# A graph kernel with three edits: early roots in the opening, late statistics in the node stage, whole rows in the last stage

## The chip, the cores and the metric

The kernel runs on one core of a Trainium2 chip. The metric is the device time of one execution in microseconds; lower is better. The kernel before was timed three times: 1190.2, 1192.75 and 1195.69 us, median 1192.75 us. Nothing in the text below is a time of the changed kernel.

The core has five engines that run programs of their own and meet at semaphores: TensorE (PE), VectorE (DVE), ScalarE (ACT), GpSimd (POOL) and SyncE (SP). SP here only issues transfers; ACT and GpSimd issue some too. All transfers share 16 DMA engines. `then_inc` raises a semaphore when an instruction is done, `wait_ge` holds the engine's program until a semaphore has reached a value.

## What is computed

`x` has 10,000 nodes of 512 columns, and there are 10,000 edges `src`, `dst` with a weight each. Two layers follow one another, each with a residual and a layer norm (`eps` 1e-5, no scale):

```python
# layer 0: graph convolution with self loops
deg = segment_sum(w, dst) + 1;  d = where(deg > 0, rsqrt(deg), 0)
agg[dst] += x[src] * d[src] * w;  z = agg + x * d          # (aggregated before the product with W)
x1 = layernorm(x + relu((z @ W0) * d + b0))
# layer 1: message passing; an edge takes x1[dst], adds into node src
sj, vj = x1[dst, :128] @ Win_s, x1[dst, 128:].reshape(-1, 128, 3) @ Win_v
u = edge_vec / |edge_vec|;  Yv = Y1 * u
filt = (shifted_softplus(edge_attr @ Wf1 + bf1) @ Wf2 + bf2) * w
# messages: scalar and vector parts from sj, vj, Yv and filt, summed over the edges of a node
S = shifted_softplus(segment_sum(m_s) @ W1_s) @ W2_s;  V = segment_sum(m_v) @ W1_v @ W2_v
out = layernorm(x1 + concat(S, V))
```

## The kernel before, in words

Nodes and edges are padded to 10,240, that is 80 tiles of 128 (`T`), 40 pairs (`T2`), 20 groups of four (`T4`). The five engine programs are written by hand, without a planner; the order of the work is the order of the lines in each program and the waits in them. A function `nodes0(s, u)` is one turn `s` of a stage on one engine, and `live(s, k)` marks the part of it that treats tile `s - k`, so a tile passes through an engine's parts in different turns. `skewed` runs the turns: some unrolled ones, then a hardware loop (`Fori`), then the tail. `held` is a wait with a mark, `Stage` counts marks of one tile.

**Opening.** SP loads the indices and weights (L332 to L346) and the first feature tiles (L353). ACT issues 42 transfers of zeros into `sum0` (L509), 512 KB each, and only then copies `W0h` (L513) and takes the roots of the degrees and of |r|^2 (L515, L516). DVE builds one-hot tiles whose products on TensorE are the degrees (L944), then runs a chain of small dependent steps (`link`): the degrees (L733 to L735), scaled weights, and after ACT's roots the reciprocals, one Newton step and `Y` (L746 to L753). Only then `s_dis` is raised. TensorE waits for it ahead of everything in the edge stage.

**Edge stage 0** (20 groups). GpSimd gathers rows of `x` by `src` (L429). TensorE transposes index columns into rows (L968), DVE compares (L774, L779, L787), picks `d[src]` from a lookup (L1023, L765) and makes `coef`; ACT scales the gathered rows into the high part `G_hi` (L559), DVE makes the low part `G_lo` (L799), TensorE sums rows with equal `dst` in a group (L984), ACT copies the sums out (L544), and GpSimd scatters them with add into `sum0` (L449) at indices from L804. The filter network of layer 1 runs beside it (L1019, L995, L538; written to `filt_d` by SP, L357). The first scatter waits for all 42 transfers of zeros, a group's scatters for those of the group before.

**Node stage** (80 tiles, `nodes0` on each engine). SP loads a tile of `sum0` (`sl`, 4 buffers) and of `x` (`xl`, 8 buffers). DVE: `z = x*d + sum` (L829). ACT: high part (L607). GpSimd: low part (L476). TensorE: four transposes of each part by `ident_r` (L1047). ACT: two copies from PSUM (L595, L600). TensorE: twelve matmuls with `W0h`, `W0l` (L1057). DVE: `*d + b0` (L823), ReLU and residual (L832), statistics (L834, L836), all one after the other on one tile. ACT: Ln and Exp of the variance (L590, L598). GpSimd: five one-column steps (L463 to L472). ACT: normalisation in place (L611). SP: two stores, `x1_d` and columns 128 to 511 of `sum1`. The result buffers `res` are four. ACT also issues zeros for the first 128 columns of `sum1`, and four last ones (L616).

**Edge stage 1** is not touched but for the buffers that it shares.

**Last stage** (40 pairs, `nodes1`). SP loads columns 0 to 127 of `sum1` for two tiles into `ssum` (L402), the other columns into `al` (L410), 128 columns of `x1_d` into `xs` (L412). `pair_rows` puts row `p` of tile `2s` and row `p` of tile `2s+1` on partition `p`. ACT and DVE compute the shifted softplus (L668, L678, L686; L900, L908), TensorE transposes and multiplies (L1121, L1128), DVE adds (L916) and takes statistics (L924, L928), ACT normalises (L657), SP stores 512 KB (L406). `al` has 8 buffers, `ssum` and `xs` 4.

## Time and profile before

| | |
|---|---|
| median of 3 runs | 1192.75 us |
| the profiled execution's own time | 1193.07 us |
| its span | 1191.3 us |
| busy: PE, DVE, ACT, POOL | 1000.9, 835.9, 701.7, 660.3 us |
| opening and edge stage 0 | 0 to 354.7 us |
| node stage, and the fill of edge stage 1 | 354.7 to 686.5 us |
| edge stage 1 | 686.5 to 1044.1 us |
| last stage | 1044.1 to 1191.3 us |
| moved by DMA | 289.00 MB, mean 243 GB/s |

The span is what the profiler saw from the first to the last instruction; the execution's own time has 1.8 us around it. A busy share is an average over stages of different kind, so it says little on what a change of one stage is worth: a stage is read by the period with which its instructions repeat, and by what each waits for. A row of the timeline has start, duration, engine, line, operation, and in brackets the idle time in front and what ended it. PE is TensorE's matmuls; PEclk is the granted share of its clock.

### The profile page before, as it was taken

Reading aid. Unit: us, or ns where it says so; the run is one execution under the profiler, and the core shown is the slowest. Engines: PE = TensorE matmul, PEld = TensorE weight load, DVE = VectorE, ACT = ScalarE, POOL = GpSimd, SP = SyncE. Lnnn points to the kernel's source line nnn. Section 1 sums busy time; section 2 is a strip of 40 time slices with the busy share of each in tenths; the row PEclk is TensorE's granted clock in tenths of the full one; section 3 lists DMA queues with packets and bytes.
Section 4 is the critical chain, followed back from the end, with each engine's and each line's share of the span. In section 5 each row is a group of like instructions: output and inputs, shape, how many; then the busy total and the mean of one; then the engine's idle time right before and its main releaser. Section 6 shows DMA issues by size and latency. Waiting matters only on the chain.

```text
span 1191.3 us, 23227 instructions
## 1 busy us (share of the span) xinstructions
PE 1000.9 (84%) x5088; PEld 790.9 (66%) x5088; DVE 835.9 (70%) x2538; ACT 701.7 (59%) x1632; POOL 660.3 (55%) x812
## 2 busy tenths in 40 slices
PE   7479998998838999999999399999999999634442
PEld 7458777776627888888888267777777777433332
DVE  8578876787606777787777366666666666368887
ACT  0068787777725666666666344444444444268887
POOL 3038888888745777777777546656566664400000
PEclk9999988999878999999999789999999999955555
DMA  9949999999986788878887669999999998589998
GB/s 356 418 156 235 245 228 229 247 253 227 220 170 207 265 276 279 277 277 278 278 277 263 235 161 211 194 202 195 205 194 208 195 205 177 69 256 347 351 351 287
DMA packets 175015, 289.00 MB, mean 243 GB/s; under 512 B 18514, under 2 KB 75750, under 8 KB 174966
## 3 DMA queue, kind: packets, MB, share of 16 engines
q1 hardware_dynamic: 120982, 176.23, 44.2%
q0 software_dynamic: 35840, 83.91, 36.7%
q10 hardware_dynamic: 18144, 28.32, 6.3%
q8 instruction: 17, 0.28, 0.1%
q14 instruction: 32, 0.26, 0.1%
HBM read 139.49 MB, written 148.90 MB: 242 GB/s over the span
## 4 chain that ended last, share of the span: by engine, by line
PE 30%; issue 17%; POOL 11%; DMA 5%; DVE 2%; ACT 2%; POOLq 2%; SPq 1%; ACTq 0%; DVEq 0%
PE bank L1084 6%; PE bank L1095 4%; POOL tiny L463 3%; PE bank L1093 3%; POOL tiny L466 3%; PE bank L1105 3%; PE bank L1107 3%; PE bank L1108 3%; DMA node_mem<-sum 3%; PE bank L1077 2%; PE bank L1085 1%; PE bank L1091 1%; PE bank L1057 1%; POOL tiny L470 1%; POOL tiny L468 1%
## 5 line engine op out<-in xcount | busy, mean ns | idle before, releaser
L500 POOL DMA_INDIRECT sum<-R_mem,l_sidx x80 | 128.0, 1600 | 126.1 <-ACT R_mem L625 74.3
L449 POOL DMA_INDIRECT sum<-R_mem,sidx_all x80 | 133.6, 1670 | 53.1 <-issue 29.1
L1057 PE MATMUL bank<-W0h,G_hi 128*128 128x512 f32 x320 | 134.0, 419 | 1.0 <-ACT G_lo L600 0.9
L1057 PE MATMUL bank<-W0l,G_hi 128*128 128x512 f32 x320 | 126.2, 394 | 0.0
L1057 PE MATMUL bank<-W0h,G_lo 128*128 128x512 f32 x320 | 126.2, 394 | 0.0
L611 ACT ACTIVATE node_mem<-node_mem,tiny 128x512 f32<-128x512 f32 x80 | 65.4, 818 | 91.7 <-POOL tiny L472 91.7
L476 POOL TENSOR_TENSOR G_lo<-node_mem,G_hi 128x512 fp32r<-128x512 f32 x80 | 104.4, 1305 | 17.8 <-ACT G_hi L607 17.8
L880 DVE SCALAR_TENSOR_TENSOR edge_mem<-edge_mem,Y,bank 128x128 f32<-128x128 f32 x240 | 72.5, 389 | 57.4 <-ACT edge_mem L639 57.4
L639 ACT COPY edge_mem<-bank 128x256 f32<-128x256 f32 x80 | 29.9, 373 | 134.3 <-PE bank L1095 134.3
L984 PE MATMUL bank<-G_hi,M_mem 128*128 128x512 f32 x200 | 88.5, 442 | 17.8 <-ACT R_mem L544 17.6
L492 POOL DMA_INDIRECT G_mem<-x_d,dst_i x80 | 79.5, 993 | 35.3 <-issue 23.2
L823 DVE SCALAR_TENSOR_TENSOR node_mem<-bank,dis,b_s 128x512 f32<-128x512 f32 x80 | 60.1, 751 | 54.1 <-DMA sum<-node_mem 46.3
L1121 PE MATMUL bank<-ident,node_mem 128*128 128x128 f32 x80 | 27.4, 446 | 83.8 <-DVE node_mem L908 83.8
L829 DVE SCALAR_TENSOR_TENSOR node_mem<-G_mem,dis,node_mem 128x512 f32<-128x512 f32 x80 | 67.0, 839 | 32.1 <-DMA G_mem<-x 32.1
L1084 PE MATMUL bank<-edge_mem,Winv 128*128 128x512 f32 x160 | 82.9, 600 | 0.5 <-DVE edge_mem L871 0.5
L984 PE MATMUL bank<-G_lo,M_mem 128*128 128x512 f32 x200 | 82.8, 414 | 0.0
L995 PE MATMUL bank<-edge_mem,Wf_s 128*128 128x256 f32 x320 | 81.0, 399 | 1.5 <-DVE edge_mem L808 0.8
L1077 PEld LDWEIGHTS bank<-ident,G_mem 128*128 128x128 f32 x240 | 40.1, 195 | 58.6 <-issue 58.6
L1121 PEld LDWEIGHTS bank<-ident,node_mem 128*128 128x128 f32 x80 | 11.6, 204 | 96.0 <-ACT node_mem L664 52.3
L995 PEld LDWEIGHTS bank<-edge_mem,Wf_s 128*128 128x128 f32 x320 | 65.7, 208 | 13.6 <-issue 2.5
L633 ACT COPY edge_mem<-bank 128x512 f32<-128x512 f32 x80 | 46.9, 587 | 42.1 <-PE bank L1079 42.1
L538 ACT ACTIVATE node_mem<-bank,bf_c 128x256 f32<-128x256 f32 x160 | 63.3, 491 | 14.3 <-PE bank L995 14.2
(172 smaller groups left out, 2953.0 us busy)
## 6 DMA issues: line engine op xcount, KB each, us to landing
sum<-zeros ACTq DMA_DIRECT2D x42, 512.0 KB, 13.7
filt_d<-node_mem SPq DMA_DIRECT2D x40, 512.0 KB, 5.1
node_mem<-sum SPq DMA_DIRECT2D x80, 256.0 KB, 2.8
G_mem<-x SPq DMA_DIRECT2D x80, 256.0 KB, 2.8
x_d<-node_mem SPq DMA_DIRECT2D x80, 256.0 KB, 2.1
node_mem<-filt_d SPq DMA_DIRECT2D x80, 256.0 KB, 4.6
sum<-node_mem SPq DMA_DIRECT2D x80, 192.0 KB, 2.3
out<-G_mem SPq DMA_DIRECT2D x20, 512.0 KB, 4.2
```

Of the source, the lines that this page charges most:

```text
L449: pool.indirect_dma_start(sum0, bass.IndirectOffsetOnAxis(ap=sidx[:, t:t + 1], axis=0), R[t % 8][:, :], None, compute_op=ALU.add).then_inc ...
L476: pool.tensor_tensor(z_lo[u][:, :], sl[u], z_hi[u][:, :].bitcast(F32), ALU.subtract).then_inc(n_lo, 1)
L492: pool.indirect_dma_start(G3[t % 8][:, :], None, x1_d, bass.IndirectOffsetOnAxis(ap=dst_i[:, t:t + 1], axis=0)) \
L500: pool.indirect_dma_start(sum1, bass.IndirectOffsetOnAxis(ap=l1_sidx[:, t:t + 1], axis=0), R3[t % 8][:, :], None, compute_op=ALU.add).then ...
L611: act.activation(res[a], res[a], ACT.Identity, bias=tiny[a][:, 6:7], scale=tiny[a][:, 5:6]) \
L829: dve.scalar_tensor_tensor(sl[c], xl[u], dis[:, bass.ds(s, 1)], sl[c], ALU.mult, ALU.add).then_inc(n_z, 1)
L880: st.mark(dve.scalar_tensor_tensor(mo[:, :, i], msg[c][:, 0:P], Y[:, bass.ds(t, 1), i], bank[6][:, i * P:(i + 1) * P], ALU.mult, ALU.add))
L984: ins = pe.matmul(bank[b][:, :], M[c][q][:, j * P:(j + 1) * P], part_[(4 * g + q) % 8][:, :], start=(q == 3 and part_ is G_hi), stop=(q == ...
L995: ins = pe.matmul(bank[6 + r][:, q * 256:(q + 1) * 256], Wf2_s[:, base:base + 255:2], h[c][:, v * 256:(v + 1) * 256], start=True, stop=True)
L1057: ins = pe.matmul(bank[4 + a][:, :], zt[b][:, c * P:(c + 1) * P], w[:, c, :], start=(c == 0 and k == 0), stop=(c == 3 and k == 2))
L1077: pe.transpose(bank[0][:, i * P:(i + 1) * P], gv[:, :, i], ident[:, :])
L1084: pe.matmul(bank[2][:, :], Winv[:, :], rawT[b][:, 0:512], start=True, stop=True)
```

## The change

Three parts, which touch separate stages.

1. Opening and edge stage 0. ACT issues 8 of the 42 transfers of zeros; SP issues the other 34, behind its loads and the first two feature tiles. ACT waits for the degrees only (`s_const` 4) before the first root. DVE takes the scaled weights and `Y` out of the opening and puts them behind the edge loop; the inverse root follows the first group's counts; TensorE waits for `s_dis` only before the first lookup. In group 0 TensorE and ACT do the first two sums ahead of the next transposes, and DVE makes `M` and `G_lo` ahead of the counts. Gathers share a semaphore by four.
2. Node stage. `z` is transposed once, in fp32; the split into high and low part is made after it (ACT `zT_hi`, DVE `zT_lo`), in four buffers each. ReLU goes to ACT, the residual add to GpSimd, and DVE's statistics follow two turns later. The tail of the statistics (Ln, Exp, GpSimd's steps) runs once for two tiles. Eight `res` buffers, eight store semaphores.
3. Last stage. `node_pair` puts rows `2p` and `2p+1` of 256 on partition `p`, so both are 4 KB in one piece; whole rows of `sum1` go into `al`, whose columns 0 to 127 take the place of `ssum`. `al` has 13 buffers, `xs` 8. Padding rows are neither loaded nor stored. All programs of the stage are unrolled, and a store stands ten turns behind its load.

```diff
+def node_pair(dram, s, c0, c1):
+
+    n = min(256, N - s * 256)
+    return dram[s * 256:s * 256 + n, c0:c1].rearrange("(p k) d -> p k d", k=2)
...
-        al = split(views(0, 4, 2 * D, G_mem) + views(0, 4, 2 * D, R_mem))
-
-        ssum, sr, sp, spT, xs = (split([b[:, q * 2 * C:(q + 1) * 2 * C] for b in node_mem]) for q in range(5))
+        NA = 13
+        al = split(views(0, 4, 2 * D, G_mem) + views(0, 4, 2 * D, R_mem) + views(0, 5, 2 * D))
+
+        sr, sp, spT = (split([b[:, q * 2 * C:(q + 1) * 2 * C] for b in node_mem]) for q in (1, 2, 3))
+        xs = split([b[:, q * 2 * C:(q + 1) * 2 * C] for q in (0, 4) for b in node_mem])
...
+            for s in range(2):
+                sp_.dma_start(fT[s][:, :], rbf[:, s * Q:(s + 1) * Q]).then_inc(w_fT[s], 16)
+            sp_.wait_ge(s_zero, 1)
+            for j in range(NZ, 42):
+                sp_.dma_start(zero_rows(j), zeros[:, :]).then_inc(s_zero0, 16)
...
-                if live(s, 8):
-                    t = s - 8
+                if live(s, 12):
+                    t, a = s - 12, (u - 12) % 8
                     held(sp_, n_x1, t + 1)
...
+            for s in range(T2 + 10):
+                if s < T2:
+                    if s >= NA:
+                        sp_.wait_ge(g_st[(s - NA) % 8], 16 * ((s - NA) // 8 + 1))
+                    if s >= 8:
+                        sp_.wait_ge(g_res, K_RES4 * (s - 8) + 1)
+                    sp_.dma_start(pairs_in(al[s % NA], s), node_pair(sum1, s, 0, D)).then_inc(g_al[s % 8], 16)
+                    sp_.dma_start(pairs_in(xs[s % 8], s), node_pair(x1_d, s, 0, C)).then_inc(g_xs[s % 8], 16)
+                if s >= 10:
+                    t = s - 10
+                    sp_.wait_ge(g_y, 2 * (t + 1))
+                    sp_.dma_start(node_pair(out, t, 0, D), pairs_in(al[t % NA], t)).then_inc(g_st[t % 8], 16)
...
+                if live(s, 7) and u % 2 == 0:
+
+                    t, a = s - 8, u // 2
+                    g = t // 2 if isinstance(t, int) else (t - u) // 2 + a
+                    w, mean, var = tiny[a], mv[a][:, :, 0], mv[a][:, :, 1]
+                    st = Stage(n_rstd, g, K_ROOT)
+                    held(pool, n_mv, t + 2)
+                    st.mark(pool.tensor_scalar(w[:, 0, :], var, EPS, None, ALU.add))
+                    st.mark(pool.tensor_scalar(w[:, 7, :], mean, -1.0, None, ALU.mult))
+                    held(pool, n_rs, 2 * (g + 1))
+                    st.mark(pool.tensor_tensor(w[:, 3, :], w[:, 2, :], w[:, 2, :], ALU.mult))
+                    st.settle(pool)
+                    st.mark(pool.tensor_tensor(w[:, 4, :], w[:, 3, :], w[:, 0, :], ALU.mult))
                     held(pool, n_rstd, st.reached())
-                    held(pool, n_rs, 2 * (t + 1))
-                    st.mark(pool.tensor_scalar(w[:, 3:4], w[:, 2:3], w[:, 2:3], w[:, 0:1], ALU.mult, ALU.mult))
-                    held(pool, n_rstd, st.reached())
-                    st.mark(pool.tensor_scalar(w[:, 4:5], w[:, 3:4], -0.5, 1.5, ALU.mult, ALU.add))
+                    st.mark(pool.tensor_scalar(w[:, 3, :], w[:, 4, :], -0.5, 1.5, ALU.mult, ALU.add))
                     st.settle(pool)
-                    st.mark(pool.tensor_tensor(w[:, 5:6], w[:, 4:5], w[:, 2:3], ALU.mult))
-                    held(pool, n_rstd, st.reached())
-                    st.mark(pool.tensor_scalar(w[:, 6:7], mean, w[:, 5:6], -1.0, ALU.mult, ALU.mult))
-                if live(s, 0):
-                    pool.wait_ge(n_hi, s + 1)
-                    wait(pool, n_tr, s - 3)
-                    pool.tensor_tensor(z_lo[u][:, :], sl[u], z_hi[u][:, :].bitcast(F32), ALU.subtract).then_inc(n_lo, 1)
-
-            skewed(pool, nodes0, 6, 8)
-
-
-            for u in range(4):
-                held(pool, n_st[u], 32 * (T // 4))
+                    st.mark(pool.tensor_tensor(w[:, 5, :], w[:, 3, :], w[:, 2, :], ALU.mult))
+                    st.settle(pool)
+                    st.mark(pool.tensor_tensor(w[:, 6, :], w[:, 7, :], w[:, 5, :], ALU.mult))
+                if live(s, 4):
+                    t, a = s - 4, (u - 4) % 8
+                    pool.wait_ge(n_rel, t + 1)
+                    pool.tensor_tensor(res[a], res[a], xl[a], ALU.add).then_inc(n_sum, 1)
+
+            skewed(pool, nodes0, 9, 16, unroll=8)
...
-            with act.Fori(0, 42) as j:
-                act.dma_start(sum0[bass.ds(j * 256, 256), :].rearrange("(p r) d -> p (r d)", r=2), zeros[:, :]) \
-                   .then_inc(s_zero0, 16)
+            for j in range(NZ):
+                act.dma_start(zero_rows(j), zeros[:, :]).then_inc(s_zero0, 16)
             act.wait_ge(s_wres, 64)
             for c in range(4):
                 act.copy(W0h[:, c, :], W0_s[c]).then_inc(s_whi, 1)
-            act.wait_ge(s_const, 11)
+            act.wait_ge(s_const, 4)
             act.activation(degs[:, :], degm[:, :], ACT.Sqrt).then_inc(s_sqrt, 1)
+            act.wait_ge(s_const, 6)
...
+                if s == 2:
+                    sums_out(0, 3, 0)
+                    sums_out(1, 2, 1)
...
+                tail = live(s, 7) and u % 2 == 0
+                if tail:
+                    t, a = s - 8, u // 2
+                    g = t // 2 if isinstance(t, int) else (t - u) // 2 + a
+                    act.wait_ge(n_mv, t + 2)
+                    act.activation(tiny[a][:, 1, :], mv[a][:, :, 1], ACT.Ln, bias=eps_c[:, :]).then_inc(n_rs, 1)
                 if live(s, 2):
-                    b, t2 = u % 2, s - 2
-                    act.wait_ge(n_tr, s - 1)
-                    wait(act, n_mm, s - 3)
-                    act.copy(zT_hi[b][:, :], bank[b][:, :]).then_inc(n_zT, 1)
-                if live(s, 5):
-                    act.wait_ge(n_rs, 2 * t + 1)
-                    act.activation(tiny[a][:, 2:3], tiny[a][:, 1:2], ACT.Exp, scale=-0.5).then_inc(n_rs, 1)
-                if live(s, 2):
-                    act.copy(zT_lo[b][:, :], bank[2 + b][:, :]).then_inc(n_zT, 1)
+                    t2, b = s - 2, (u - 2) % 4
+                    act.wait_ge(n_tr, t2 + 1)
+                    wait(act, n_mm, t2 - 3)
+                    act.copy(zT_hi[b][:, :], bank[b][:, :]).then_inc(n_hi, 1)
                     act.dma_start(sum1[bass.ds(t2 * P, P), 0:C], zeros[:, 0:C]).then_inc(s_zero1, 16)
-                if live(s, 0):
-                    a = u % 4
-                    act.wait_ge(n_z, s + 1)
-                    wait(act, n_tr, s - 3)
-                    wait(act, n_lo, s - 3)
-                    act.copy(z_hi[a][:, :], sl[a]).then_inc(n_hi, 1)
-                if live(s, 6):
-                    t, a = s - 6, (u - 6) % 4
-                    act.wait_ge(n_rstd, K_ROOT * (t + 1))
-                    act.activation(res[a], res[a], ACT.Identity, bias=tiny[a][:, 6:7], scale=tiny[a][:, 5:6]) \
+                if tail:
+                    act.wait_ge(n_rs, 2 * g + 1)
+                    act.activation(tiny[a][:, 2, :], tiny[a][:, 1, :], ACT.Exp, scale=-0.5).then_inc(n_rs, 1)
+                if live(s, 4):
+                    t4, c = s - 4, (u - 4) % 8
+                    act.wait_ge(n_pre, t4 + 1)
+                    act.activation(res[c], res[c], ACT.Relu).then_inc(n_rel, 1)
+                if live(s, 9):
+                    t8, c = s - 9, (u - 9) % 8
+                    k, b = c % 2, c // 2
+                    g8 = t8 // 2 if isinstance(t8, int) else (t8 - c) // 2 + b
+                    act.wait_ge(n_rstd, K_ROOT * (g8 + 1))
+                    act.activation(res[c], res[c], ACT.Identity, bias=tiny[b][:, 6, k:k + 1], scale=tiny[b][:, 5, k:k + 1]) \
                        .then_inc(n_x1, 1)
 
-            skewed(act, nodes0, 6, 8, unroll=8)
+            skewed(act, nodes0, 9, 16, unroll=8)
...
+            def inverse_root():
+                dve.wait_ge(s_sqrt, 1)
+
+                link(dve.reciprocal(dis[:, :], degs[:, :]))
+                link(dve.tensor_tensor(degt[:, :], degt[:, :], dis[:, :], ALU.mult))
+                link(dve.tensor_tensor(degt[:, :], degt[:, :], dis[:, :], ALU.mult))
+                link(dve.tensor_scalar(degt[:, :], degt[:, :], -0.5, 1.5, ALU.mult, ALU.add))
+                link(dve.tensor_tensor(dis[:, :], dis[:, :], degt[:, :], ALU.mult))
+                link(dve.tensor_tensor(dis[:, :], dis[:, :], deg[:, :], ALU.mult))
+                dve.sem_inc(s_dis, 1)
...
+                if s == 0:
+                    counts1()
+                    inverse_root()
+                if s >= 2:
+                    counts0()
+                    if s < T4:
+                        counts1()
...
+                    if s == 1:
+                        counts0()
+                        counts1()
...
-                if live(s, 4):
-                    t, a = s - 4, (u - 4) % 4
-                    st = Stage(n_res, t, K_RES)
-                    dve.wait_ge(n_mm, t + 1)
-                    wait(dve, n_st[a], 32 * turn(t, a, 4))
-
-                    st.mark(dve.scalar_tensor_tensor(res[a], bank[4 + a][:, :], dis[:, bass.ds(t, 1)], b0_s[:, :],
-                                                     ALU.mult, ALU.add))
                 if live(s, 0):
                     c = u % 4
                     dve.wait_ge(n_sl[c], 16 * (turn(s, c, 4) + 1))
                     dve.wait_ge(n_xl[u], 16 * (turn(s, u, 8) + 1))
                     dve.scalar_tensor_tensor(sl[c], xl[u], dis[:, bass.ds(s, 1)], sl[c], ALU.mult, ALU.add).then_inc(n_z, 1)
+                if live(s, 6):
+                    t, c, a = s - 6, (u - 6) % 4, (u - 6) % 8
+                    dve.wait_ge(n_sum, t + 1)
+                    dve.bn_stats(stat[c][:, :], res[a]).then_inc(n_bn, 1)
+                if live(s, 2):
+                    t, b = s - 2, (u - 2) % 4
+                    dve.wait_ge(n_hi, t + 1)
+                    wait(dve, n_mm, t - 3)
+                    dve.tensor_tensor(zT_lo[b][:, :], bank[b][:, :], zT_hi[b][:, :].bitcast(F32), ALU.subtract).then_inc(n_lo, 1)
+                if live(s, 6):
+                    t, a = s - 6, (u - 6) % 8
+                    k, b = a % 2, a // 2
+                    if k == 0:
+                        held(dve, n_x1, t - 6)
+                    held(dve, n_bn, t + 1)
+                    dve.bn_aggr(mv[b][:, k, :], stat[a % 4][:, :]).then_inc(n_mv, 1)
                 if live(s, 4):
-                    st.settle(dve)
-                    st.mark(dve.scalar_tensor_tensor(res[a], res[a], 0.0, xl[(u - 4) % 8], ALU.max, ALU.add))
-                    st.settle(dve)
-                    st.mark(dve.bn_stats(stat[a][:, :], res[a]))
-                    held(dve, n_res, st.reached())
-                    st.mark(dve.bn_aggr(mv[a][:, :], stat[a][:, :]))
-
-            skewed(dve, nodes0, 4, 8, unroll=8)
+                    t, c, a = s - 4, (u - 4) % 4, (u - 4) % 8
+                    dve.wait_ge(n_mm, t + 1)
+                    wait(dve, n_st[a], 32 * turn(t, a, 8))
+                    dve.scalar_tensor_tensor(res[a], bank[4 + c][:, :], dis[:, bass.ds(t, 1)], b0_s[:, :],
+                                             ALU.mult, ALU.add).then_inc(n_pre, 1)
+
+            skewed(dve, nodes0, 6, 16, unroll=8)
...
+                if live(s, 1):
+                    t, a = s - 1, (u - 1) % 4
+                    pe.wait_ge(n_z, t + 1)
+                    wait(pe, n_lo, t - 3)
+                    for c in range(4):
+                        ins = pe.transpose(bank[a][:, c * P:(c + 1) * P], sl[a][:, c * P:(c + 1) * P], ident[:, :])
+                    ins.then_inc(n_tr, 1)
...
-                        for k, (zt, w) in enumerate(((zT_hi, W0h), (zT_hi, W0l), (zT_lo, W0h))):
-                            ins = pe.matmul(bank[4 + a][:, :], zt[b][:, c * P:(c + 1) * P], w[:, c, :],
-                                            start=(c == 0 and k == 0), stop=(c == 3 and k == 2))
+                        for w in (W0h, W0l):
+                            pe.matmul(bank[4 + a][:, :], zT_hi[a][:, c * P:(c + 1) * P], w[:, c, :],
+                                      start=(c == 0 and w is W0h), stop=False)
+                    pe.wait_ge(n_lo, t + 1)
+                    for c in range(4):
+                        ins = pe.matmul(bank[4 + a][:, :], zT_lo[a][:, c * P:(c + 1) * P], W0h[:, c, :],
+                                        start=False, stop=(c == 3))
                     ins.then_inc(n_mm, 1)
```

## Rows read from the trace of the kernel before

**Rows 1.** windows by stage: stretch, length, busy us per engine, PEclk, DMA share, GB/s

```profile
354.70:686.50 331.80, 303.90 (x1600) 259.54 (x1601) 240.58 (x403) 208.45 (x482) 234.15 (x487) 0.95 0.77 264
...
1044.07:1191.30 147.23, 61.94 (x240) 49.91 (x240) 120.27 (x480) 118.19 (x320) 0.00 (x0) 0.50 0.97 321
```

**Rows 2.** timeline of the opening, 40 to 95 us: start, duration, engine, line, operation

```profile
43.96 0.20 DVE L734 TENSOR_SCALAR degm<-deg 128x80 f32<-128x80 f32 x1
...
61.54 0.27 ACT L515 ACTIVATE degs<-degm 128x80 f32<-128x80 f32 x1
...
62.11 0.65 DVE L746 RECIPROCAL dis<-degs 128x80 f32<-128x80 f32 x1 [16.08 <-ACT rn L516]
...
66.68 1.12 PE L968 MATMUL bank<-ident,dst_f 128*128 128x128 f32 x4 [3.14 <-DVEq L755]
...
73.56 0.30 DVE L765 SCALAR_TENSOR_TENSOR junk<-iota_f,part,bank 128x80 f32<-128x80 f32 x1 [2.48 <-PE bank L1023]
...
83.19 0.16 DVE L804 TENSOR_TENSOR sidx_all<-off_all,dst_f 128x4 int32<-128x4 f32 x1
...
88.96 1.86 POOL L449 DMA_INDIRECT sum<-R_mem,sidx_all  x1 [18.68 <-ACT R_mem L544]
```

**Rows 3.** the zeros' issues on ACT: ns min/median/max, first and last start, landing; a window

```profile
L509 ACTq DMA_DIRECT2D sum<-zeros x42: 366/855/2132, 2.2 to 55.7; - x42
...
DMA to landing us min/median/max: 4.0/13.7/15.5
...
20.00:40.00 20.00, 20.00 (x95) 20.00 (x95) 20.00 (x95) 0.00 (x0) 0.00 (x0) 1.00 1.03 414
```

**Rows 4.** timeline of GpSimd, first scatters of two following groups

```profile
237.60 1.62 POOL L449 DMA_INDIRECT sum<-R_mem,sidx_all  x1 [0.30 <-issue]
...
250.89 1.62 POOL L449 DMA_INDIRECT sum<-R_mem,sidx_all  x1 [0.30 <-issue]
```

**Rows 5.** timeline of GpSimd in the node stage, and all instances of L463

```profile
503.35 0.52 POOL L463 TENSOR_SCALAR tiny<-mv 128x1 f32<-128x1 f32 x1
...
505.72 1.31 POOL L476 TENSOR_TENSOR G_lo<-node_mem,G_hi 128x512 fp32r<-128x512 f32 x1
...
507.12 0.52 POOL L463 TENSOR_SCALAR tiny<-mv 128x1 f32<-128x1 f32 x1
...
L463 POOL TENSOR_SCALAR tiny<-mv x80: 209/526/728, 376.9 to 669.9; 128x1 f32<-128x1 f32 x80
```

**Rows 6.** timeline of TensorE in the node stage; a step of the chain in edge stage 1

```profile
503.30 0.56 PE L1047 MATMUL bank<-ident_r,G_hi 128*128 128x128 f32 x4
...
504.21 0.50 PE L1057 MATMUL bank<-W0h,G_hi 128*128 128x512 f32 x1
...
1015.85 0.34 PE bank L1077 x3
```

**Rows 7.** timeline of ACT and DVE in the node stage, and all instances of L829

```profile
502.04 0.82 ACT L611 ACTIVATE node_mem<-node_mem,tiny 128x512 f32<-128x512 f32 x1 [1.19 <-POOL tiny L472]
...
502.76 0.28 ACT L590 ACTIVATE tiny<-mv,eps_c 128x1 f32<-128x1 f32 x1
...
502.94 0.57 ACT L595 CAST G_hi<-bank 128x512 fp32r<-128x512 f32 x1
...
502.26 0.75 DVE L823 SCALAR_TENSOR_TENSOR node_mem<-bank,dis,b_s 128x512 f32<-128x512 f32 x1 [0.54 <-DMA sum<-node_mem]
...
502.93 0.88 DVE L829 SCALAR_TENSOR_TENSOR node_mem<-G_mem,dis,node_mem 128x512 f32<-128x512 f32 x1
...
L829 DVE SCALAR_TENSOR_TENSOR node_mem<-G_mem,dis,node_mem x80: 740/789/1744, 358.5 to 654.0; 128x512 f32<-128x512 f32 x80
```

**Rows 8.** windows and DVE's L916 in the last stage

```profile
1080.00:1100.00 20.00, 8.74 (x36) 7.03 (x35) 17.55 (x72) 16.95 (x48) 0.00 (x0) 0.50 1.06 353
...
1081.86 0.42 DVE L916 TENSOR_TENSOR G_mem<-bank,node_mem 128x256 f32<-128x256 f32 x1
...
1085.05 0.42 DVE L916 TENSOR_TENSOR G_mem<-bank,node_mem 128x256 f32<-128x256 f32 x1
```

210 lines of the change are left out of this document (90 added, 120 removed).

## The prediction

> **What bounds the kernel now.** I read the windows first, then the timeline of one steady tile in each stage that the change touches, then the instances of single lines. The kernel is four stages with a barrier of transfers between them. Two of them are in [rows 1]: the node stage (354.7 to 686.5, with the fill of the stage behind it) and the last stage (1044.07 to 1191.3, 147.2 us). In no stage is one engine plainly full, so I looked for what repeats once a period.
>
> Opening and first edge stage: the degrees are ready at 44.2, but the square root runs at 61.54, TensorE's first transposes start at 66.68, the first lookup is picked at 73.56, the first group's scatter indices come at 83.35 and the first scatter at 88.96 [rows 2]. ScalarE is late because it issues all 42 transfers of zeros, the last at 55.7 [rows 3]. From 88.96 on the stage is GpSimd's: one group of four tiles (four scatters, four gathers, 0.30 us between) takes 250.89 - 237.60 = 13.29 us [rows 4], and all other engines wait now and then. So the start of the first scatter is passed on to the end of the stage one for one.
>
> Node stage: GpSimd repeats every 507.12 - 503.35 = 3.77 us without waiting for another engine: five tiny operations and the 1.30 us subtraction for z_lo [rows 5]. TensorE repeats in the same time; 0.91 us of it are the eight transposes (503.30 to 504.21), the rest twelve matmuls of 0.23 us a step [rows 6]. Both are at the limit, GpSimd a little more.
>
> Last stage: DVE repeats every 85.05 - 81.86 = 3.19 us when it isn't starved; the stretch 1080 to 1100 moves 353 GB/s at a DMA share of 1.06 [rows 8]. A pair of tiles moves 1.18 MB (640 KB in, 512 KB out), 3.34 us at 353 GB/s. So here transfers are the limit, and DVE is close behind.
>
> **The opening.** ScalarE issues 8 zero transfers instead of 42 and is free for the weights and the roots; SP issues the other 34 behind the loads. The root can start at 44.2 + 0.1 + a table load of some 1.3 = 45.6. TensorE may then start after ScalarE's two small copies; between 0.6 and the 5.1 us of before (61.54 to 66.68) I take 2.5: 48.1. From first transposes to first pick took 6.88 us, and the inverse root, 66.68 - 62.11 = 4.57 with the reciprocal and the product for Y, 3.4 without them, now stands in front of the lookup [rows 2]: 48.1 + 6.9 + 3.4 = 58.4. Pick to indices took 9.79 us; DVE does the same instructions in another order (M and G_lo ahead of the counts), so 68.2, and one compare more in front, 69. The sums go ahead of the next group's transposes on TensorE, so they are there before the indices, unlike now (5.6 us after).
>
> The other condition of the first scatter is that all zeros have landed. Their bytes don't shrink. The last one is issued at 55.7 and the median to landing is 13.7: 69.4 [rows 3]. The stream already moves 414 GB/s at a share of 1.03, so it can't get shorter; four gathers of 0.26 MB are pulled in front of its end (1.05 MB / 414 GB/s = 2.5 us at most), and if SP leaves a gap between its loads and the zeros it gets longer. I take 70. Gain: 89 - 70 = **19 us**; bounds 9 (zeros 10 us late) and 21. Behind the zeros in SP's queue now stands the third feature tile, for which TensorE waits ahead of the fourth sum of group 0: landing at some 71 to 72, it is needed at about 71. I cost it at 0; without this cover it delays one scatter by 1 to 3 us, inside the bounds. The 34 zeros cost SP's queue nothing else, since it stood idle. Moving Y, 1/|r| and the weight scalings to the end of the edge loop costs DVE some 2 us where it waits for the last scatter: 0. One semaphore per four gathers: the last gathered tile was waited for first anyway, 0.
>
> **The node stage.** Per tile: four fp32 transposes for eight; ScalarE makes zT_hi (0.57) and a ReLU, no z_hi and no copy of zT_lo; DVE makes zT_lo from PSUM in place of the ReLU-add; GpSimd makes the residual add in place of z_lo, and the statistics' tail once per two tiles. Floors: TensorE 3.76 - 0.91 + 0.45 = 3.30, or less 0.05 for the semaphore, 3.25 (three such transposes take 0.34 [rows 6]). GpSimd: 1.30 + half of a chain of seven tiny ones, which was 2.4 for five (503.35 to 505.72) and is some 3.1 for seven, gives 2.9. DVE about 3.0. ScalarE 2.6.
>
> The limit that I expect is none of these but a ring of waits through two engines, closed once per tile. In DVE's program zT_lo(t) stands ahead of the bias step of tile t-2, in ScalarE's the ReLU and the normalisation stand ahead of the next zT_hi; ReLU waits for the bias step, zT_lo for zT_hi. Round: bias step 0.75, hand-over 0.05, ReLU 0.53 (nearest row: the copy of such a tile from PSUM, 0.57; somewhat more from SBUF, less the 0.1 by which a following instruction starts before its end), normalisation 0.72 (502.04 to 502.76), half an Ln 0.09 (0.18 per pair), zT_hi 0.57, hand-over 0.10, zT_lo 0.60 (nearest row: the bias step, which also reads PSUM), aggregate 0.12 [rows 7] = 3.53, and 0.02 for the loop's turn: **3.55 us**. Bounds: TensorE's 3.25 if the pieces overlap more, and 4.35 (rival 4). Gain 80 x (3.76 - 3.55) = **17 us**. At the head one step of 1.30 (z_lo) goes off the way to the first matmul, at the tail an add of 1.30 is put on the way to the last normalisation: 0 together. Eight `res` buffers and the store's old 4-deep wait: covered by three periods, 0.
>
> **The last stage.** Rows in and out are 4 KB pieces, two neighbouring rows a partition, only 128 columns of x1 stay 512 B; the separate 128 KB load of the sums' scalar part goes. At the stream's 414 GB/s [rows 3] 1.05 MB take 2.53 us, the 0.13 MB in small pieces at 353 GB/s 0.37: 2.90 us a pair, under DVE's 3.19. So DVE sets the pace: 3.34 - 3.19 = 0.15 us off each of some 35 steady pairs = 5.3 us. The first pair waits for 512 KB instead of 128 KB: +1.2. The last pair is 16 rows, the padding isn't moved: -1.5. Loop registers are gone and the ring is 13 deep: up to 1 us. Sum **-6 us**; bounds 0 and -10.
> By the Trainium skill (DMA: Bandwidth & Descriptors, section Bandwidth) HBM gives one core some 358 GB/s. Then a pair would take 3.29 us and the stage would gain 2 us, not 5.3, before the ends; the 414 GB/s of the zeros, which are HBM writes, speaks against it here.
>
> **Sum.** 19 + 17 + 6 = 42 us. The profiled execution took 1193.07 us (span 1191.3 and 1.8 around it), 0.3 over the median 1192.75. 1193.07 - 42 = **1151 us**.
>
> **Rivals.**
> 1. The ring doesn't bind, and TensorE does, at 3.25 us: 80 x 0.30 = 24 us more off, **1127**. For it: the starts of most instructions overlap by 0.1, and TensorE has no idle in the stage now. Against it: the ring's waits follow from program order alone.
> 2. The node stage gains nothing (3.76: GpSimd or the ring at the old pace): **1168**. For it: GpSimd's tiny operations last 0.53 where the shortest lasts 0.21 [rows 5].
> 3. The change doesn't do in the opening what it says: the zeros, issued from SP behind the loads, land 8 us later and hold the first scatter: **1159**. For it: the stream is saturated and has more in front; against: 8 zeros, the loads and eight gathers fill its first 20 us.
> 4. Slower. The one mechanism: GpSimd's add and DVE's z step hold each other up. Both read two SBUF tiles. The z step lasts 740 to 1744 ns (median 789) and a one-column GpSimd operation 209 to 728 [rows 5, 7]; those long ones stand beside such DVE steps. If each z step met the add, it would take up to 1.0 to 1.3 us more; 0.5 of it is DVE's slack in the ring, the rest goes into it: 3.55 + 0.8 = 4.35. 80 x 0.59 = 47 us on, 25 off: **1215**. It decides from a period of 4.08. Against: in the ring the add starts when the z step has just ended, and one of the two DVE steps with two SBUF inputs is gone.
> This is what the Trainium skill (SBUF — State Buffer, on the shared port pair) calls an exclusive lock between GpSimd and a DVE operation with two SBUF inputs: the loser blocks for the whole instruction. The trace agrees, the operation from 503.35 ends at 503.88, the z step beside it (502.93, 0.88 long) at 503.81 [rows 5, 7].
>
> **Chances.** Forecast (ring, 3.4 to 3.7) 0.45, own range 1140 to 1163; rival 1 0.23; rival 2 0.13; rival 3 0.11; rival 4 0.05; something unseen 0.03. The range 1125 to 1172 leaves out rival 4 and the lower tail of rival 1. About 0.5% (6 us) is what a measurement tells from no change: only rival 4 and part of the unseen are slower, 0.05; within 0.02; faster 0.93.
>
> **What would show it.** Opening: root at 45 to 47, first scatter at 69 to 71, last zero landed just before; then groups of 13.3. Node stage: a period of 3.55 with ScalarE idle before the ReLU (released by DVE) and DVE idle before zT_lo (released by ScalarE); TensorE with gaps. No gaps on TensorE at 3.25 is rival 1; z steps over 1.2 us are rival 4. Last stage: DVE at 3.2 without stalls on loads, 138 to 143 us long. The prediction is wrong if first scatters wait past 75, or if the node period leaves 3.4 to 3.7.

## The result, and the profile after

The changed kernel takes **1145.43 us** (median of 4 runs, 1142.33 to 1147.13) against 1192.33 for the kernel before on the same chip: ratio 0.9601, 95% interval 0.957 to 0.9632, 47 us less. The forecast was 1151. The stages add up to it, but not each with the size that was forecast:

| stage | before | after | gain | forecast |
|---|---|---|---|---|
| opening and edge stage 0 (to the first load of the node stage) | 354.69 | 339.81 | 14.9 | 19 |
| node stage with its tail (to the first gather of the next) | 323.98 | 293.64 | 30.3 | 17 |
| edge stage 1 | 365.40 | 366.04 | -0.6 | 0 |
| last stage | 147.23 | 144.61 | 2.6 | 6 |
| span | 1191.3 | 1144.1 | 47.2 | 42 |

The gains by stage come from one profiled execution of each kernel. The limits of the stages are starts of rows such as these, from GpSimd's and SP's timeline of the changed kernel (start, duration, engine, line, operation, idle time in front and what ended it):

```profile
73.62 1.74 POOL L462 DMA_INDIRECT sum<-R_mem,sidx_all  x1 [34.88 <-DMA sum<-zeros]
...
87.07 1.75 POOL L462 DMA_INDIRECT sum<-R_mem,sidx_all  x1 [0.30 <-issue]
...
339.81 0.35 SPq L386 DMA_DIRECT2D node_mem<-sum  x1
```

The first scatter starts at 73.62, not at 88.96 [rows 2], and the bracket names its releaser: the last zeros. The windows in front of it show how they end (us, busy us and instructions of PE, PEld, DVE, ACT, POOL, then clock, DMA share, GB/s):

```profile
70.00:71.00 1.00, 1.00 (x6) 0.91 (x5) 0.84 (x7) 0.82 (x2) 0.00 (x0) 0.50 0.51 201
...
72.00:73.00 1.00, 1.00 (x7) 0.86 (x6) 1.00 (x5) 1.00 (x3) 0.00 (x0) 1.00 0.06 25
```

At full rate the stream ends soon after 70, but a share of 0.06, about one of the 16 DMA engines, goes on for two more microseconds. By the trace's packets the last 4 KB packet of zeros ends at 72.84, where that of the kernel before ended at 69.70. From the first scatter on the first group takes 87.07 - 73.62 = 13.45 us, about as before [rows 4]. The steps between root and scatter, from the timelines of ScalarE, TensorE and DVE:

```profile
47.80 0.20 DVE L755 TENSOR_SCALAR degm<-deg 128x80 f32<-128x80 f32 x1
...
48.04 0.27 ACT L531 ACTIVATE degs<-degm 128x80 f32<-128x80 f32 x1 [18.02 <-DVE degm L755]
...
51.02 1.12 PE L1011 MATMUL bank<-ident,dst_f 128*128 128x128 f32 x4 [0.54 <-ACT MV L540]
...
59.16 0.30 DVE L798 SCALAR_TENSOR_TENSOR junk<-iota_f,part,bank 128x80 f32<-128x80 f32 x1 [1.75 <-PE bank L1072]
...
68.80 0.16 DVE L833 TENSOR_TENSOR sidx_all<-off_all,dst_f 128x4 int32<-128x4 f32 x1
```

The degrees are 3.8 us later than before (43.96 [rows 2]), although their own steps were not changed. The window 20 to 40 us shows where (columns as above), and behind it rows of the timelines there:

```profile
20.00:40.00 20.00, 16.54 (x75) 16.11 (x75) 20.00 (x76) 3.46 (x5) 8.76 (x8) 1.00 1.03 406
```

```profile
28.52 0.31 DVE L746 TENSOR_SCALAR hot_hi<-iota_f,part,ew 128x80 f32<-128x80 f32 x1
28.76 1.38 DVE L744 TENSOR_SCALAR hot_lo<-iota_f,part 128x128 f32<-128x128 f32 x1
28.80 4.93 POOL L450 TENSOR_TENSOR W0l<-node_mem,W0h 128x512 fp32r<-128x512 f32 x4 [12.82 <-ACT W0h L529]
...
33.70 0.27 DVE L744 TENSOR_SCALAR hot_lo<-iota_f,part 128x128 f32<-128x128 f32 x1
```

DVE finishes 76 instructions of the one-hot loop there instead of 95 [rows 3]. ScalarE now copies the weights early, so GpSimd's four subtractions for `W0l` and four gathers fall into this loop; before they came after it. The subtractions are the cause. While they run, DVE does four one-hot steps of 1.27 to 1.38 us each, one for each subtraction of 1.26, and right behind the last one a step is back at 0.27. ScalarE's copies in front of them (26.54 to 28.72) and the gathers behind them cost nothing: DVE does 20 steps in the 4 us from 34 to 38, as in the 4 us from 24 to 28. Runs 6 and 7 below, in which ScalarE issues all zeros again and copies the weights late, have 95 instructions in this window again, and this step on the degrees starts at 43.55 and 43.47. So a part of the change itself (early weights) took back 3.8 us of the early root. By which means the two engines hold each other up no run here separates.

In the node stage two views show the limit. The waits of the window 400 to 600 (engine, line, releaser: us in total, times, longest):

```profile
ACT node_mem L626 <- DVE node_mem L880: 84.5, 59, 1.5
POOL node_mem L493 <- ACT node_mem L626: 52.4, 29, 1.8
DVE G_lo L868 <- ACT G_hi L618: 41.2, 59, 0.8
```

And the timeline of DVE and ScalarE for two turns:

```profile
500.17 0.56 ACT L618 CAST G_hi<-bank 128x512 fp32r<-128x512 f32 x1
...
502.23 0.63 ACT L626 ACTIVATE node_mem<-node_mem 128x512 f32<-128x512 f32 x1 [1.40 <-DVE node_mem L880]
...
502.77 0.80 ACT L632 ACTIVATE node_mem<-node_mem,tiny 128x512 f32<-128x512 f32 x1
503.47 0.56 ACT L618 CAST G_hi<-bank 128x512 fp32r<-128x512 f32 x1
...
504.07 0.69 DVE L868 TENSOR_TENSOR G_lo<-bank,G_hi 128x512 fp32r<-128x512 f32 x1 [0.61 <-ACT G_hi L618]
504.68 0.17 DVE L875 BATCH_NORM_AGGREGATE mv<-stat 128x2 f32<-128x6 f32 x1
504.76 0.72 DVE L880 SCALAR_TENSOR_TENSOR node_mem<-bank,dis,b_s 128x512 f32<-128x512 f32 x1
...
505.52 0.63 ACT L626 ACTIVATE node_mem<-node_mem 128x512 f32<-128x512 f32 x1 [1.48 <-DVE node_mem L880]
506.05 0.80 ACT L632 ACTIVATE node_mem<-node_mem,tiny 128x512 f32<-128x512 f32 x1
506.76 0.28 ACT L613 ACTIVATE tiny<-mv,eps_c 128x2 f32<-128x2 f32 x1
506.95 0.56 ACT L618 CAST G_hi<-bank 128x512 fp32r<-128x512 f32 x1
```

Read it as a circle from 503.47 on (L618, ScalarE's `zT_hi`): each row starts when the one above lets it, and with the eighth row the first line comes again. ScalarE idles 1.4 us before the ReLU, DVE 0.6 before zT_lo, GpSimd before its add, and the circle sets the period, 503.47 - 500.17 = 3.30 us in a turn without Ln, 506.95 - 503.47 = 3.48 in one with it, 3.385 in the mean over 39 turns. Only TensorE looks full:

```profile
400.00:600.00 200.00, 199.79 (x959) 159.51 (x958) 158.71 (x296) 115.04 (x235) 129.07 (x266) 1.00 0.95 310
```

Its 199.79 of 200 us say less than they seem to. Matmuls are pipelined and their ends are modelled, so short gaps vanish in this column; run 1 passes 1001 instead of 959 of them through the same window at the same granted clock, 1.00, and shows 200.00.

In the last stage the same picture appears, which the forecast had not drawn. One turn of ScalarE and of DVE:

```profile
1073.88 0.40 ACT L707 ACTIVATE node_mem<-node_mem 128x256 f32<-128x256 f32 x1
...
1074.37 0.42 DVE L953 TENSOR_TENSOR node_mem<-node_mem 128x256 f32<-128x256 f32 x1 [0.17 <-DVE node_mem L945]
1074.71 0.15 DVE L956 SCALAR_TENSOR_TENSOR tiny<-tiny 128x2 f32<-128x2 f32 x1
1074.79 0.42 DVE L960 TENSOR_TENSOR R_mem<-bank,node_mem 128x256 f32<-128x256 f32 x1
1075.12 0.15 DVE L964 SCALAR_TENSOR_TENSOR tiny<-mv,tiny 128x2 f32<-128x2 f32 x1
...
1075.30 0.81 ACT L678 ACTIVATE R_mem<-R_mem,tiny 128x512 f32<-128x512 f32 x1 [0.36 <-DVE tiny L964]
1076.02 0.40 ACT L699 ACTIVATE node_mem<-node_mem 128x256 f32<-128x256 f32 x1
1076.33 0.19 ACT L702 ACTIVATE tiny<-tiny 128x2 f32<-128x2 f32 x1
1076.42 0.80 ACT L678 ACTIVATE R_mem<-R_mem,tiny 128x512 f32<-128x512 f32 x1
1077.13 0.40 ACT L707 ACTIVATE node_mem<-node_mem 128x256 f32<-128x256 f32 x1
```

L953 needs ScalarE's Ln (L707), which ends at 1074.28, 0.09 before it starts; the bracket names DVE's own L945, whose result only the next turn reads. That the Ln is what it waits for is a reading of the program here; runs 8 and 11 test it. Closed over ScalarE (0.49 + 0.34 + 0.08 + 0.33 + 0.18 + 0.72 + 0.31 + 0.09 + 0.71) the circle is 3.25 us, exactly the period. No load is waited for any more.

### The profile page after: what moved, and what is told of

It reads as the page before. It is cut to its first block, busy times and chain, and to the rows that moved or that the text cites. A ratio compares the mean times of both kernels' runs of the same rounds, so it can differ in the third digit from the quotient of the medians.

```text
span 1144.1 us, 20007 instructions
## 1 busy us (share of the span) xinstructions
PE 963.5 (84%) x4768; PEld 744.5 (65%) x4768; DVE 812.6 (71%) x2537; ACT 651.0 (57%) x1472; POOL 602.4 (53%) x692
## 4 chain that ended last, share of the span: by engine, by line
PE 37%; ACT 10%; issue 9%; DVE 7%; DMA 3%; ACTq 2%; POOL 1%; DVEq 1%; SPq 1%; POOLq 0%
PE bank L1133 6%; PE bank L1144 5%; PE bank L1102 4%; DVE node_mem L880 3%; PE bank L1142 3%; PE bank L1154 3%; PE bank L1156 3%; PE bank L1157 3%; PE bank L1126 2%; ACT G_hi L618 2%; PE bank L1106 2%; ACTq L619 2%; ACT node_mem L632 2%; PE bank L1134 2%; PE bank L1140 2%
## 5 line engine op out<-in xcount | busy, mean ns | idle before, releaser
L462 POOL DMA_INDIRECT sum<-R_mem,sidx_all x80 | 130.9, 1636 | 71.4 <-DMA sum<-zeros 34.9
L493 POOL TENSOR_TENSOR node_mem<-node_mem,G_mem 128x512 f32<-128x512 f32 x80 | 103.2, 1290 | 91.7 <-ACT node_mem L626 91.7
L626 ACT ACTIVATE node_mem<-node_mem 128x512 f32<-128x512 f32 x80 | 50.7, 633 | 118.1 <-DVE node_mem L880 118.1
L868 DVE TENSOR_TENSOR G_lo<-bank,G_hi 128x512 fp32r<-128x512 f32 x80 | 55.2, 691 | 52.4 <-ACT G_hi L618 52.3
L1106 PE MATMUL bank<-W0h,G_lo 128*128 128x512 f32 x320 | 86.6, 393 | 0.0
L859 DVE SCALAR_TENSOR_TENSOR node_mem<-G_mem,dis,node_mem 128x512 f32<-128x512 f32 x80 | 59.4, 743 | 33.5 <-DMA G_mem<-x 33.4
L1102 PEld LDWEIGHTS bank<-W0h,G_hi 128*128 128x128 f32 x320 | 60.6, 189 | 19.7 <-ACT G_hi L618 4.5
L912 DVE TENSOR_TENSOR edge_mem<-node_mem,bank 128x256 f32<-128x256 f32 x80 | 33.6, 421 | 54.4 <-issue 28.4
```

Of the source, the lines that this page charges most:

```text
L462: pool.indirect_dma_start(sum0, bass.IndirectOffsetOnAxis(ap=sidx[:, t:t + 1], axis=0), R[t % 8][:, :], None, compute_op=ALU.add).then_inc ...
L493: pool.tensor_tensor(res[a], res[a], xl[a], ALU.add).then_inc(n_sum, 1)
L859: dve.scalar_tensor_tensor(sl[c], xl[u], dis[:, bass.ds(s, 1)], sl[c], ALU.mult, ALU.add).then_inc(n_z, 1)
L1102: pe.matmul(bank[4 + a][:, :], zT_hi[a][:, c * P:(c + 1) * P], w[:, c, :], start=(c == 0 and w is W0h), stop=False)
L1106: ins = pe.matmul(bank[4 + a][:, :], zT_lo[a][:, c * P:(c + 1) * P], W0h[:, c, :], start=False, stop=(c == 3))
```

## Experiments

A batch of runs shares a chip. The end of edge stage 0 lies between 335.2 and 344.2 us in the eleven profiles that have the changed opening, so across batches lengths of stages are compared, and totals only inside a batch. A part of this spread is in the opening: in all four profiles of the first batch the degrees come at 52.3 to 52.5 instead of 47.8, and the first scatter, at 74.3 to 74.8, is released by its indices and not by the zeros. What delays DVE there (it waits 4.1 us for TensorE in the one-hot loop of run 1) stays open. The rest is in the groups behind: with the same code on one chip the end still differs by up to 3 us (runs 5 and 8 to 10).

**1. Is it a ring? Take the normalisation out of it.** First batch, with the next three. The theory: the node stage's ring; the rival: TensorE or transfers.

```diff
-  ReLU of tile t-4 (waits for the bias step);  normalisation of tile t-9
+  normalisation of tile t-9;  ReLU of tile t-4 (waits for the bias step)
```

> In ScalarE's turn of the node stage the normalisation of tile t-9 is put ahead of the ReLU of tile t-4, where ScalarE waits for DVE anyway. Theory (the ring of waits zT_hi, zT_lo, aggregate, bias step, ReLU, normalisation sets the measured period of 3.39 us): 0.70 us leave the ring, 2.7 are left, and TensorE becomes the limit at its floor of some 3.25. 80 x 0.14 = 11 us less than the changed kernel, 1134 us, and DVE hardly waits for zT_hi any more. Rival (3.39 is TensorE's own time with its semaphores, or the transfers'): no change, 1145 us.

Measured: 1134.59 us, ratio to before 0.9532 (0.9498 to 0.9566), 12.9 us under run 3 of the same batch. That the total meets the theory's 1134 is partly luck: the stage gains 12.8 us, more than the 11 expected, and the opening is slower on this chip. Period 3.197 us over 39 turns, node stage 280.9 us (293.6). Its waits of DVE, 400 to 600 us:

```profile
DVE node_mem L880 <- PE bank L1106: 23.9, 61, 0.5
...
DVE G_lo L868 <- ACT G_hi L618: 0.8, 1, 0.8
```

DVE no longer waits for ScalarE (once in 61 turns) but for TensorE, 0.4 us a tile: the ring is gone and TensorE's floor is reached, 0.05 us under my estimate of it. Its matmuls start every 0.23 us and its transposes every 0.11, without a gap from one tile to the next. No transfer is among the waits.

**2 and 3. Lengthen the ring, and put the same work beside it.**

```diff
 # run r_in
   wait for the bias step of t-4
+  ReLU of 128x512 zeros into an unused buffer
   ReLU of tile t-4
 # run r_out
+  ReLU of 128x512 zeros into an unused buffer
   wait for the bias step of t-4
   ReLU of tile t-4
```

> One more ReLU of 128x512 (zeros into a buffer that nobody reads) in each turn of the node stage on ScalarE, behind the wait for the bias step, so inside the supposed ring. Theory (ring): the period grows by the whole start-to-start time of a ReLU, 0.53 us: 80 x 0.53 = 42 us, 1188 us. Rival (TensorE sets the pace, ScalarE has 0.8 us of slack a tile): at most 5 us, 1145 to 1150.

> The same extra ReLU one line earlier, ahead of the wait for the bias step, where ScalarE idles 1.40 us a tile. Theory (ring): hidden, 0 to 2 us, 1145 to 1147. Rival (ScalarE's own sum of work decides): as with the extra ReLU behind the wait, 1188.

Measured: 1184.55 us behind the wait (0.9959, 0.9941 to 0.9977), 1147.5 ahead of it (0.9646, 0.9614 to 0.9679). Same instruction, one line apart, 37 us apart. The periods are 3.907 and 3.383 us, the node stages 331.6 and 293.3. The instruction that stands behind the wait in each (in run 2 it is the added ReLU):

```profile
505.21 0.64 ACT L626 ACTIVATE edge_mem<-zeros 128x512 f32<-128x512 f32 x1 [1.48 <-DVE node_mem L881]
```

```profile
502.80 0.63 ACT L627 ACTIVATE node_mem<-node_mem 128x512 f32<-128x512 f32 x1 [0.95 <-DVE node_mem L881]
```

Inside the ring it adds 0.52 us a tile and the idle 1.48 stays; outside it only eats the idle (0.95 left) and costs nothing. The 0.52 us are the theory's; the stage grew by 38 and the total by 37, not by 42, since the period holds for the middle of the stage and its first and last turns grew less. With run 1 this shows the ring.

**4. Node stage undone.**

```diff
-  nodes0 of the changed kernel on all five engines, its buffers and semaphores
+  nodes0 of the kernel before (z_hi, z_lo, eight transposes, statistics per tile)
```

> The changed kernel with the node stage of before (z_hi, z_lo, eight transposes, statistics per tile), the new opening and the new last stage kept. Theory (the node stage is worth the 80 x 0.37 = 29.6 us that its period shows): 1145.4 + 30 = 1175 us, period 3.76. Rival (part of the gain comes from the parts together, such as the other buffers): 1160 to 1168.

Measured: 1178.06 us (0.9905, 0.9872 to 0.9937), period 3.78, stage 325.7 us against 293.6, 32 us; the total lies 30.6 over run 3 of the same batch. The theory holds: the gain belongs to the node stage alone. DVE's z step, all instances from 400 to 600 us (ns minimum, median, maximum), in this kernel and in the changed one:

```profile
L864 DVE SCALAR_TENSOR_TENSOR node_mem<-G_mem,dis,node_mem x52: 741/852/1227, 402.9 to 596.3; 128x512 f32<-128x512 f32 x52
```

```profile
L859 DVE SCALAR_TENSOR_TENSOR node_mem<-G_mem,dis,node_mem x59: 739/743/752, 400.5 to 596.9; 128x512 f32<-128x512 f32 x59
```

**5. Fewer zeros.** Second batch, with the next two. The 42nd and 41st transfers write only rows that nobody reads as results.

```diff
-  for j in range(NZ, 42): ...;  wait_ge(s_zero0, 16 * 42)
+  for j in range(NZ, 40): ...;  wait_ge(s_zero0, 16 * 40)
```

> 40 transfers of zeros instead of 42 in the opening; the last 512 rows of the first buffer of sums (only trash rows, which nothing reads, and no node's) stay unwritten. Theory (the first scatter, at 73.6 in the changed kernel, waits for the stream of zeros, which moves 418 GB/s): 1.05 MB less, so 2.5 us earlier: first scatter 71.1, total 1143. Rival (the first scatter hangs on something else, such as the scatter indices at 68.8 or the first sums): no change, 1145.4.

Measured: 1145.44 us (0.9607, 0.9576 to 0.9638), nothing gained, though the interval, some 4 us to either side, could not show 2.5 us. Its trace can. First, third and fourth scatter, and the first of the next group:

```profile
70.85 1.60 POOL L462 DMA_INDIRECT sum<-R_mem,sidx_all  x1 [32.18 <-DMA sum<-zeros]
...
75.48 1.54 POOL L462 DMA_INDIRECT sum<-R_mem,sidx_all  x1 [0.82 <-ACT R_mem L561]
78.84 1.89 POOL L462 DMA_INDIRECT sum<-R_mem,sidx_all  x1 [1.82 <-ACT R_mem L561]
...
86.22 1.75 POOL L462 DMA_INDIRECT sum<-R_mem,sidx_all  x1 [0.30 <-issue]
```

The first scatter moves by 2.77 us as expected, so the zeros do hold it here. But the third and fourth scatter then wait 0.82 and 1.82 us for their sums, and the second group starts only 0.85 us earlier than 87.07. The theory was right on the first scatter and wrong on what it is worth: the limits lie close together. The first batch shows the third of them, the indices, in front, with all 42 zeros (run 1):

```profile
74.80 1.60 POOL L462 DMA_INDIRECT sum<-R_mem,sidx_all  x1 [36.09 <-DVE sidx_all L833]
```

**6. All zeros from ScalarE again.**

```diff
-  NZ = 8
+  NZ = 42
```

> All 42 zero transfers issued by ScalarE again (none by SP), everything else as in the changed kernel. Theory (early roots are worth what the first scatter would lose without them): the root falls back from 48.0 to some 61.5, the indices come 20.8 us later, 82.3, and the first scatter with them at 82.4: 8.8 us late, total 1154. So of the opening's 15 us about 9 come from who issues the zeros, 6 from the shorter way from root to indices (before: 61.54 to 83.35 and 5.6 more to the scatter). Rival (the root isn't on the path, the zeros are in both cases): 1145 to 1147.

Measured: 1155.98 us (0.9703, 0.9674 to 0.9732), 10.5 more than with 40 zeros on the same chip. The first scatter:

```profile
83.13 1.60 POOL L462 DMA_INDIRECT sum<-R_mem,sidx_all  x1 [12.98 <-DVE sidx_all L833]
```

It comes 9.5 us later than in the changed kernel and its releaser is now the indices. The theory (8.8 later) holds. So who issues the zeros is some 10 of the opening's 15 us.

**7. Opening undone.**

```diff
-  the changed opening (8 + 34 zeros, inverse root behind the first counts, sums ahead of transposes)
+  the opening of before
```

> The changed kernel with the opening of before (zeros all from ScalarE, roots and Y before the edge stage, order of counts and sums of before); only the gathers' shared semaphores stay. Theory (parts add up): first scatter at 89, 15 us more, 1160 us. Rival (the shared semaphore or later stages take part): off by more than 3 us from 1160.

Measured: 1158.45 us (0.9718, 0.969 to 0.9746), first scatter at 88.75, 13 us over the run with 40 zeros. Parts add up within 2 us. The 2.5 us over run 6 are what the rest of the opening's edits is worth, where the text of run 6 had put 6.

**8. DVE's work to GpSimd.** Third batch, with the next two. What limits the last stage: DVE or the transfers?

```diff
-  DVE:    sr = max(s, 0) - log 2          (128x256, one a pair)
+  GpSimd: sr = max(s, 0) - log 2
```

> In the last stage the step max(s, 0) - log 2 (0.29 us, 128x256) goes from DVE to GpSimd, which is idle there. Theory A (DVE sets the pace of 3.25 us a pair): the step's 0.2 us and the 0.17 wait behind it leave DVE's turn, up to 0.35 us, until the stream (at 414 GB/s 2.9 us) or DVE's 2.9 binds: 35 x 0.3 = 10 us less, 1135; 3 us if GpSimd holds DVE up. Theory B (1.18 MB a pair at some 362 GB/s, 3.25 us, is the limit of the transfers, and DVE follows it): no change, 1145, and DVE waits for loads.

Measured: 1146.12 us (0.9614, 0.9589 to 0.9639), period 3.343 instead of 3.252. Theory A fails. Its waits, 1020 to 1120 us:

```profile
DVE node_mem L955 <- ACT node_mem L712: 8.2, 28, 0.3
```

With L945's work gone from DVE, the wait stays and the bracket now names ScalarE's Ln. That led to the ring of the section above. The ring also accounts for the 0.09 us that the period grew. One of its small DVE steps now stands beside GpSimd's 1.07 us operation:

```profile
1077.41 0.24 DVE L966 SCALAR_TENSOR_TENSOR tiny<-mv,tiny 128x2 f32<-128x2 f32 x1
```

It is L964 of the changed kernel, which took 0.15 us there.

**9. Fewer bytes.** The rows of `x1` are loaded for the first eight pairs only; the output is not the reference's.

```diff
-  xs load for every pair
+  if s < 8: xs load
```

> The loads of the 128 columns of x1 (0.13 MB a pair, pieces of 512 bytes) are left out from the ninth pair on; the sums then use old rows, so the output is not the reference's. Theory A (DVE sets the pace): no change, 1145. Theory B (transfers): 0.13 of 1.18 MB less in 32 pairs, 0.36 us each, 11 us less until DVE's own turn binds: 1135 to 1143.

Measured: 1144.78 us (0.9593, 0.9568 to 0.9618), period 3.251 as in the changed kernel, and this window (columns as above):

```profile
1020.00:1120.00 100.00, 47.79 (x186) 38.67 (x186) 89.60 (x370) 88.85 (x247) 0.00 (x0) 0.50 0.89 311
```

The stream falls from 351 GB/s in the same window of the changed kernel to 311, the pace doesn't change: theory B fails too. This run alone would fit theory A; with run 8 neither is left, which is how a ring looks when one asks for a full engine.

**10. Last stage undone.**

```diff
-  whole rows, two neighbours a partition, 13 deep, no loops
+  last stage of before
```

> The changed kernel with the last stage of before (row p of two tiles on partition p, scalar columns loaded for themselves, hardware loops, 8 buffers), the rest kept. Theory (the last stage is worth the 2.6 us that the two traces show): 1148 us. Rival (the old mapping costs more than that or nothing here): 1145 or over 1151.

Measured: 1149.05 us (0.9636, 0.9612 to 0.966; in its batch 4.3 over run 9), stage 147.9 us against 144.6, period 3.39 against 3.25 (1020 to 1120 us). The stage's length fits the theory; the totals lie too close together to tell it from 1151. By lengths of stages the three parts undone add up to 32.1, 13.3 (the end of edge stage 0 in runs 7 and 5) and 3.3 us, 48.7 for the 47.2 that they gave together.

**11. Break the last stage's ring.** Fourth batch, with the next.

```diff
-  normalise(1);  Ln of the softplus (waits for its Exp)
+  Ln of the softplus (waits for its Exp);  normalise(1)
```

> In ScalarE's turn of the last stage the last softplus step (Ln, 128x256) is put ahead of the second normalisation of another pair. Theory (the last stage too is a ring of waits: Ln to DVE's sum 0.49, three DVE steps 0.34 + 0.08 + 0.33, hand-over to the first normalisation 0.18, 0.72, Exp and small Exp 0.40, second normalisation 0.71 = 3.25 us, the period measured): 0.71 leave the ring, and DVE's own turn binds, 3.25 less its wait of 0.17 = 3.08. 36 x 0.17 = 6 us less than the changed kernel, 1139 us. Rival (transfers bind at the 351 GB/s of this stage): no change, 1145, and DVE's wait only moves.

Measured: 1131.65 us (0.9502, 0.9488 to 0.9516). Last stage 136.2 us against 144.6, period 3.009. The rest of the 13.8 us lies ahead of it, in stages whose code is the same (edge stage 0 ends 4.65 us earlier in this run), so 8.4 us are the edit's, where 6 were expected. A part of a turn of DVE:

```profile
1064.16 0.15 DVE L948 TENSOR_TENSOR tiny<-tiny 128x2 f32<-128x2 f32 x1
1064.23 0.42 DVE L953 TENSOR_TENSOR node_mem<-node_mem 128x256 f32<-128x256 f32 x1
```

And a window:

```profile
1060.00:1090.00 30.00, 15.35 (x62) 12.46 (x60) 28.14 (x121) 29.32 (x81) 0.00 (x0) 0.50 1.04 392
```

The wait before L953 is gone; from L948 to L953 it is 0.07 us instead of 0.32. The edit took off 0.25 a turn where the idle in the bracket said 0.17, because an unhindered instruction starts 0.08 before the end of the one in front. The rival falls as well: the stream carries 392 GB/s when the engines ask for it, 364 in the same 30 us of the changed kernel.

**12. All three orders together.**

```diff
+  node stage as in 1, last stage as in 11
+  DVE: sr put between the statistics and their aggregate, where DVE waits 0.15 us for itself
```

> The order of the last stage as in the run beside it, DVE's max(s, 0) - log 2 put between the statistics and their aggregate (where DVE waits 0.15 us for itself), and in the node stage the normalisation ahead of the ReLU. Theory: 11 us from the node stage (measured alone: 1134.6 for 1145.4), 6 from the last stage's ring and 0.15 x 36 = 5 from DVE's turn: 1123 to 1125 us. Rival (the last stage is bound by its transfers or by ScalarE's sum of 2.9 us and waits): 1134 to 1129.

Measured: **1119.09 us** (1117.78 to 1120.49), ratio 0.9396 (0.9382 to 0.9411), the best of all: by the ratios (0.9396 for 0.9601) 24 us under the changed kernel, by the medians 26. Node stage 280.2 us, last stage 134.6: together 23.4 us less than in the changed kernel, where the theory had added up 22. The rest under its range of 1123 to 1125 lies ahead, in edge stage 0, which ends 3.4 us earlier with the same code. The third order gave 0.03 us a turn (period 2.978) instead of 0.15: ScalarE, busy 29.32 of 30 us in run 11, is now busy 29.65 of them and binds.

## Why the prediction was right in direction, and where its sizes were off

**Opening, 19 forecast, 14.9 measured.** Right: the indices (69, measured 68.8), the first pick (58.4, measured 59.2), the scatter released by the last zeros, groups of 13.3 behind it in the mean, the third feature tile without cost. Wrong: "I take 70". The indices came right by errors that cancel. The root was taken at 45.6 and came at 48.0, because the degrees were taken as untouched (44.2) and GpSimd's subtractions delayed them. In return the inverse root took 2.0 us (55.43 to 57.42 in DVE's timeline) where 3.4 had been put down, and the way from pick to indices 9.6 us where 10.6 had. The zeros are the mis-sized term: my own sum of 69.4 and 2.5 for the gathers in front of the stream's end gives 71.9, and I had cut it to 70. The last packet of zeros ended at 72.84, 0.6 behind 69.70 and 2.5, and the scatter came 0.8 later, at 73.6. This is rival 3 by half, 3.6 of its 8 us. Run 5 bounds what it was worth: with the zeros out of the way the next group starts 0.85 us earlier, since the sums of the third and fourth tile come no earlier. What the forecast missed is that second limit.

**Node stage, 17 forecast, 30.3 measured.** The mechanism is the one forecast, and runs 1 to 3 show it: ScalarE waits before the ReLU and DVE before zT_lo, as the text had put it. The sizes of its pieces, start to start:

| piece | forecast | measured |
|---|---|---|
| bias step to ReLU | 0.80 | 0.76 |
| ReLU | 0.53 | 0.53 |
| normalisation | 0.72 | 0.71 |
| half an Ln | 0.09 | 0.09 |
| zT_hi to zT_lo | 0.67 | 0.60 |
| zT_lo | 0.60 | 0.61 |
| aggregate | 0.12 | 0.08 |
| loop | 0.02 | 0 |
| period | 3.55 | 3.385 |

The step that failed is the sum of durations and hand-overs: the estimated hand-overs were too long by some 0.1 together, the short operation counted with its full length although the next starts 0.08 before its end. 0.165 us too much per tile are 80 x 0.165 = 13.2 us. The rest: the period before was 3.79 in the mean over the stage's middle and not the 3.76 that the sum used (one pair of rows gave 3.77 [rows 5]), 2.4 us more gain, and head and tail cost 2 instead of 0 (293.64 - 80 x 3.385 = 22.8 against 323.98 - 80 x 3.79 = 20.8). The prediction's own sign of being wrong was a period outside 3.4 to 3.7, and by that sign it was wrong, by 0.015. Rival 1 (TensorE binds) was wrong for this kernel and right for its next step: run 1 has it at 3.20. Rival 2 falls by the period. Rival 4 didn't come: the z step lasts 739 to 752 ns in all 80 tiles, without a single long one. In the second turn shown above it ends at 506.14 and GpSimd's add starts at 506.23, behind it, as the text had argued.

**Last stage, 6 forecast, 2.6 measured.** "So DVE sets the pace" failed. 3.19 was the distance of two rows of DVE, and it was no measure of DVE's own work: in the kernel before the same circle through ScalarE is closed in that very turn.

```profile
1081.00 0.40 ACT L686 ACTIVATE node_mem<-node_mem 128x256 f32<-128x256 f32 x1
...
1081.44 0.42 DVE L908 TENSOR_TENSOR node_mem<-node_mem 128x256 f32<-128x256 f32 x1
```

The Ln ends at 1081.40, DVE's sum starts at 1081.44, and the next Ln starts at 1084.20: 3.20 us round. In the changed kernel this hand-over, start to start, is 0.49 instead of 0.44 us, and the circle 3.25; why it is longer stays open. The longer turns between, up to 3.8 us, are gone. In the mean over 35 pairs the period went from 3.352 to 3.252, 0.10 where 0.15 had been forecast, 3.5 us instead of 5.3. The first statistics come 11.1 us after the first load instead of 9.1, 2.0 for the larger first transfer where 1.2 had been put down; what is left to 2.6, 1.1 us, is the shorter end. Runs 8, 9 and 11 show why: neither DVE nor the transfers, but a second ring through ScalarE. The transfers followed the pace. By the Trainium skill (DMA: Bandwidth & Descriptors, section Bandwidth) some 358 GB/s is one core's limit from HBM; the section also calls it each core's part when both cores of a pair stream. The 351 GB/s of this stage (1020 to 1120 us) look like that limit. The 392 GB/s of run 11, with the same transfers, show that here, with one core running, it was none.

**The total** came right, 1145 for 1151, because a gain under-estimated by 13 us met two over-estimated by 4 and 3; so close a hit is luck. Edge stage 1, untouched, differs by 0.6 us. Of the signs that the text named, five were missed by a little: the root (48.0 for 45 to 47), the first scatter (73.6 for 69 to 71, though not past 75), the node period, the length of the last stage (144.6 for 138 to 143), and the gaps on TensorE, which its busy time doesn't show.

## What to carry to other kernels

When no engine is full, look for a circle: follow one tile's rows from releaser to releaser across the engines until the same line returns, and add start-to-start times, not durations. The order of two independent instructions in one program is then worth up to the length of one of them per tile, until the next limit binds (37 us here for an added ReLU of 0.53 us, one line up or down; 8.4 and 12.8 us for two swaps), while work beside the circle is free as long as its engine has idle time. A busy time of 199.8 in 200 us on TensorE did not tell that it was the limit. And when two causes are each ruled out as the limit (less work on the engine, fewer bytes), the next suspect is the order.

## What the runs showed of the hardware that was not expected

- A DVE or ScalarE instruction that waits for nobody starts about 0.08 to 0.1 us before the end recorded for the one in front (DVE 504.68, 0.17 long, followed at 504.76; ScalarE 502.23, 0.63 long, followed at 502.77). An idle time in brackets therefore understates what a wait costs: 0.17 shown, 0.25 regained in run 11.
- A bracket may name an instruction on the same engine that only happened to end nearby (L945 for L953), while the real releaser was on another (ScalarE's Ln); taking the named one away (run 8) brought the other to light.
- Four one-hot steps on DVE (0.28 and 0.32 us alone) took 1.27 to 1.38 us each while GpSimd subtracted four 128x512 tiles, 1.26 us each; beside GpSimd's gathers the steps kept their pace. Each of these DVE steps reads one tile and one or two columns, not two tiles.
- Loads and stores together ran at 392 GB/s on one core (run 11), zeros alone at 414 [rows 3].
- A stream of zeros that moved 420 GB/s until 70 us needed until 72.84 for its last packets, at a DMA share of 0.06 at the end.
